# Copying the turned maxima between the two exponentials of a unit instead of ahead of both

## The chip, the cores and the metric

The kernel runs on one core of a Trainium2 chip. The metric is the device time of one execution, in microseconds (us). The profile is that of one execution. Its engines are called PE (TensorE; PEld is its loading of weights), ACT (ScalarE), DVE (VectorE), POOL (GpSimd) and SP (the DMA queue's issuer).

## The reference

A block of attention and a block of experts, each with a residual sum. What the change touches is the attention:

```python
Q, K, V = (content @ Wq), (content @ Wk), (content @ Wv)       # 4 x 1024 x 256, in 16 heads of 16
scores = jnp.einsum('bqhd,bkhd->bhqk', Q, K) / math.sqrt(HEAD_DIM)
alpha = jax.nn.softmax(scores, axis=-1)                        # over all 1024 keys
alpha = jnp.where(causal, alpha, 0)                            # the mask comes after the softmax
Y = jnp.einsum('bhqk,bkhd->bqhd', alpha, V)
x = x + layernorm(Y)
```

After it a router picks 2 of 8 experts for each of the 4096 tokens, and each expert is a 256 to 1024 to 256 MLP with GELU.

## The kernel before

The 64 pairs of batch and head are worked off in 16 groups of 4 heads (`GH = 4`, `NGR = 16`). The program position is written `p` (one group a position) and `k` (32 units a position, `U = 32`). The work of a group is a software pipeline over three positions, and each engine has a function `body(p, u, units)` which says, unit by unit, what that engine does there. Tables such as `at_m` or `at_chunk` give the unit in which each step of a group falls, counted from the start of the group's own position; a value over 31 falls in the next position or the one after it. `due(table, k)` lists what falls in unit `k`. The engines meet by semaphores only.

In each unit, for the group of the position (the *first pass*):

- PE multiplies one block of 128 queries with all 1024 keys of a head (two matmuls, line L1266, into PSUM banks 0 to 3 in turn). It may run two units ahead of DVE (`s_max`).
- DVE reduces the 128x1024 scores to the negated maximum of each query (L1706).

After each head (every 8 units) POOL splits the 8 columns of maxima in three bf16 parts (L736 to L742, `mparts`), PE turns them (L1279, a 24x128 result in rows 96 to 119 of bank 6 or 7), **ACT copies the turned maxima to `mT`** (L910, a CAST of 24x128) and counts `s_mtc`, and POOL spreads them over 24 rows of the queries' tile (L749, counts `s_ex`). So the second pass subtracts the maximum inside the matmul. The units are `at_m = [9, 17, 25, 33]`: k = 9, 17, 25 of the group's own position and k = 1 of the next one. ACT waits for `s_mtp` (PE's turning) and `s_ex` (POOL's spreading of the head before) there.

For the group before (the *second pass*), 64 chunks of 128x512, two in each unit from k = 9 on (`at_chunk = [U + LAG_B + U * c // NCH ...]`, `LAG_B = 9`):

- PE makes chunk c in bank 4 or 5 (`ebank = 4 + c % 2`, L1079; every fourth, a *corner*, L1072). It waits until exponential c - 2 is done (`s_expB`), because the two share a bank.
- ACT takes the exponential of chunk c (L926, to `et_sb`; of a corner L921, in place, with its sum in an accumulator that is read out behind it). It waits for `s_ST` (the chunk) and `s_pv` (the buffer is free).
- Each three or so units there is a *burst* on PE (L1109): the exponentials of 4 heads times the values. Bursts stand at k = 13, 16, 18, 21, 24, 26, 29 and at k = 0, 2, 5, 8, 10 of the position after. POOL multiplies the blocks on the diagonal with the mask (L770) ahead of them.

PE's own order in a unit is: turning back of results, burst, first chunk, two matmuls of the first pass, turning of the maxima (L1279), second chunk:

```python
pieces(p, u, k)
todo = due(at_chunk, k)
chunk(p, u, *todo[0])
...                       # first pass, two matmuls
...                       # turning of the maxima
for c, back in todo[1:]:
    chunk(p, u, c, back)
```

The burst of k = 2 starts a new accumulation in the bank in which the turned maxima of k = 1 lie, and waits for `s_mtc` therefore:

```python
if i == 0 and piece == 0:
    ...
    pe.wait_ge(s_mtc, min(GH * g + M_BEFORE_PV[j], NH) if isinstance(g, int) else
               GH * g + M_BEFORE_PV[j])
```

The first chunks (8 of position 1 on) begin after the projections; positions 6 to 14 are a loop of three positions run three times, and behind position 17 come the experts, whose matmuls are L1211 and L1225. The first three copies of `mT` and that of k = 1 in position 1 stand where no chunks are due yet; the other 60 have two exponentials in their unit.

Of the kernel before, what the change touches and what calls it, by code (L numbers as in the profile page):

```python
# [5 lines left out]
def sandwich(nc, x_d, wq_d, wk_d, wv_d, router_d, wfc_d, wproj_d, out_d):  # L6

    F32, BF16, I32, U32 = mybir.dt.float32, mybir.dt.bfloat16, mybir.dt.int32, mybir.dt.uint32
    ACT = mybir.ActivationFunctionType
# [38 lines left out]
    with ctx:  # L48
        def sb(name, shape, dt=F32):
            return ctx.enter_context(nc.sbuf_tensor(name, shape, dt))  # L50

        def sem(name):
            return ctx.enter_context(nc.semaphore(name))
# [10 lines left out]
        GH = 4  # L64
        NSL = 3
# [19 lines left out]
               for s in range(HSL)]  # L85
# [5 lines left out]
        NET = 3  # L91
        w0 = 0
        et_sb = [wfc[:, w0 + s * GH * 512:w0 + (s + 1) * GH * 512].rearrange("p (h q) -> p h q", h=GH)
                 for s in range(NET)]
# [34 lines left out]
        den_u = sb("den_u", [P, NSL, GH, QT // 2])  # L129
# [87 lines left out]
        def bk(i):  # L217
            return ps[:, i, :]
# [25 lines left out]
        s_dt = sem("s_dt")  # L244
# [5 lines left out]
        s_ST = sem("s_ST")  # L250
        s_expB = sem("s_expB")
        s_mask = sem("s_mask")
        s_pv = sem("s_pv")
# [91 lines left out]
        HQ = QT // 2  # L345
        HALVES = (1, 0)
        BURSTS = tuple((i, 1) for i in range(QT)) + tuple((i, 0) for i in range(HQ))
        NBU = len(BURSTS)
        NCH = (NBU + HQ) * GH
# [15 lines left out]
        at_chunk = [U + LAG_B + U * c // NCH for c in range(NCH)]  # L365
# [6 lines left out]
        def is_corner(c):  # L372

            return c % 4 == 3
# [24 lines left out]
        def due(at, k):  # L399

            return [(n, x // U) for n, x in enumerate(at) if x % U == k]
# [5 lines left out]
        def ebank(c, g):  # L407

            if isinstance(g, int) and g == NGR - 1:
                return LAST_RING[c % 4]  # L410
            return 4 + c % 2

        def live(p, back):

            return not isinstance(p, int) or 0 <= p - back < NGR
# [43 lines left out]
        def tail(at, p, k):  # L459

            if not isinstance(p, int) or p < NGR:
                return []
            return [n for n, x in enumerate(at) if x == U * (p - NGR) + k]
# [21 lines left out]
        def wait_pos(eng, s, v):  # L485

            if isinstance(v, int) and v <= 0:
                return
            eng.wait_ge(s, v)
# [32 lines left out]
        def turn_bank(hl, g):  # L522

            return 7 if isinstance(g, int) and g == 0 else 6 + HALVES[M_HALF[hl]]
# [317 lines left out]
        def _(act):  # L842
# [37 lines left out]
            def exp_gate(i):  # L880
                g = ORDER[i]
                act.wait_ge(s_d2, i + 1)
                nc.scalar.activation(gtmp[:, g * TPC:(g + 1) * TPC], gtmp[:, g * TPC:(g + 1) * TPC],
                                     ACT.Exp).then_inc(s_ex2, 1)

            def copy_x2(i, kc):
                act.wait_ge(s_x2t, KC * i + kc + 1)
                nc.scalar.copy(x2T[:, kc, :], bk(x_bank(i, kc))).then_inc(s_x2e, 1)

            def copy_l(i):  # L890
                if i == 0:
                    act.wait_ge(s_ysz, 16 * 5)
                act.wait_ge(s_lt, i + 1)
                nc.scalar.copy(lgT[:, :], bk(0)[:, 0:P]).then_inc(s_lc, 1)

            def body(p, u, units=range(U)):
                for k in units:
                    for i in tail(at_copy_l, p, k):
                        copy_l(i)
                    for n in tail(at_copy_x, p, k):  # L900
                        copy_x2(*divmod(n, KC))
                    for i in tail(at_gate, p, k):
                        exp_gate(i)
                    for hl, back in due(at_m, k):
                        if not live(p, back):
                            continue
                        h = GH * (p - back) + hl
                        act.wait_ge(s_mtp, h + 1)
                        wait_pos(act, s_ex, h)
                        nc.scalar.copy(mT[MROW:MROW + MR, :],  # L910
                                       bk(turn_bank(hl, p - back))[MROW:MROW + MR, 0:P]).then_inc(s_mtc, 1)
                    for c, back in due(at_chunk, k):
                        if not live(p, back):
                            continue
                        g = p - back
                        act.wait_ge(s_ST, NCH * g + c + 1)
                        if is_corner(c):
                            hl, i = divmod(c // 4, HQ)
                            if c < 4:
                                wait_pos(act, s_dt, g - 2)  # L920
                            nc.scalar.activation(bk(ebank(c, g)), bk(ebank(c, g)), ACT.Exp,  # L921
                                                 accum_out=den_u[:, (u - back) % NSL, hl, i:i + 1]).then_inc(s_expB, 1)
                            continue
                        b, hl = divmod(3 * (c // 4) + c % 4, GH)
                        wait_pos(act, s_pv, NBU * g + b - NET + 1)
                        nc.scalar.activation(et_sb[b % NET][:, hl, :], bk(ebank(c, g)), ACT.Exp).then_inc(s_expB, 1)  # L926

            root_c(0, 0)
            apply_c(0, 0)
# [3 lines left out]
            for c in range(NC):  # L933
                for pos in range(PER):
# [31 lines left out]
                    for p, k in early(c, pos):  # L966
                        body(p, p % NSL, (k,))
            part1(4 * NC - 1)
            act.wait_ge(s_warm, 1)
            nc.scalar.activation(warm[:, 1:2], cst0[:, 0:1], ACT.Exp).then_inc(s_warm, 1)  # L970
            groups(act, body)


# [944 lines left out]
```

## Time and profile before

| | |
|---|---|
| time, median of 3 executions | 1563.65 us (1562.59 to 1565.73) |
| time of the profiled execution | 1563.69 us |
| its span, first to last instruction | 1561.8 us |
| PE, DVE, ACT, POOL busy | 1423.3, 923.9, 805.1, 610.7 us |
| copies to `mT` (L910) | 64, of 0.258 us |
| exponentials (L926, L921) | 768 of 0.597 us and 256 of 0.584 us |
| stretch of the 60 copies that have exponentials beside them | 155 to 919 us |

A timeline row reads: start, how long, engine, line, operation, what it writes and reads, how many instructions are merged in it, and in brackets for how long the engine sat idle ahead of it and what ended that. A row of merged instructions (x2) gives the time from the first one's start to the last one's end.

### The profile page before, as it was taken

How to read it: one execution, taken by the hardware profiler on the slowest of the kernel's cores; microseconds unless marked ns; L12 is line 12 of the kernel's file. 1: busy time of each engine (PE TensorE's matmuls, PEld its weight loads, DVE VectorE, ACT ScalarE, POOL GpSimd, SP SyncE). 2: the span in 40 equal slices, each digit the busy share in tenths (PEclk: the TensorE clock that was granted, in tenths of full speed). 3: DMA queues.
4: the chain of work that ended last, by engine and by line, in shares of the span. 5: the costliest groups of instructions: out<-in, count | busy, mean ns of one | idle time of the engine just before them, and what ended most of it. 6: DMA issues, size and time to landing. Idle time of an engine off the chain costs nothing.

```text
span 1561.8 us, 31019 instructions
## 1 busy us (share of the span) xinstructions
PE 1423.3 (91%) x9774; PEld 829.3 (53%) x9775; DVE 923.9 (59%) x1740; ACT 805.1 (52%) x1717; POOL 610.7 (39%) x729
## 2 busy tenths in 40 slices
PE   6788999999999889998999998889999999999990
PEld 3444333333333223332333333689999999999990
DVE  4587788778888878887888887861111111111115
ACT  5454777777777767776777787311111111111114
POOL 2234434444444435443544441423333333333335
PEclk9999999999999999999999999999999999999995
DMA  3666622102320221132025141556666666666646
GB/s 124 153 154 142 223 41 42 30 13 41 42 40 3 42 42 27 16 42 43 16 27 96 55 136 56 158 137 193 172 183 183 176 191 173 179 188 175 187 119 219
DMA packets 100425, 167.07 MB, mean 107 GB/s; under 512 B 12400, under 2 KB 67568, under 8 KB 100304
## 3 DMA queue, kind: packets, MB, share of 16 engines
q1 hardware_dynamic: 86192, 146.08, 35.2%
q0 software_dynamic: 13632, 18.69, 7.5%
q8 instruction: 63, 1.03, 0.3%
q10 hardware_dynamic: 480, 0.79, 0.3%
q14 instruction: 58, 0.48, 0.1%
HBM read 130.76 MB, written 34.77 MB: 106 GB/s over the span
## 4 chain that ended last, share of the span: by engine, by line
PE 66%; DVE 15%; issue 9%; ACT 4%; POOL 2%; DMA 2%; DVEq 1%; ACTq 0%; POOLq 0%
PE ps L1211 16%; PE ps L1225 15%; PE ps L1109 10%; DVE negmax L1706 9%; PE ps L1079 8%; PE ps L1266 8%; ACT wfc L926 2%; PE ps L1048 2%; PE ps L1072 2%; POOL wfc L838 1%; PE ps L1253 1%; DVE x L1524 1%; PE ps L1198 1%; ACT yx L853 1%; PE ps L1057 1%
## 5 line engine op out<-in xcount | busy, mean ns | idle before, releaser
L1706 DVE TENSOR_REDUCE negmax<-ps 128x1 f32<-128x1024 f32 x512 | 607.0, 1217 | 146.3 <-PE ps L1266 143.8
L926 ACT ACTIVATE wfc<-ps 128x512 f32<-128x512 f32 x768 | 436.6, 595 | 178.0 <-PE ps L1079 169.6
L981 ACT ACTIVATE wfc<-ps 128x512 f32<-128x512 f32 x142 | 84.8, 597 | 426.8 <-PE ps L1211 426.8
L1211 PE MATMUL ps<-yx,wfc 128*128 128x128 f32 x2272 | 267.6, 276 | 5.3 <-issue 5.3
L1211 PEld LDWEIGHTS ps<-yx,wfc 128*128 128x128 f32 x2272 | 265.8, 193 | 9.5 <-issue 6.3
L770 POOL TENSOR_TENSOR wfc<-wfc,causal 128x512 f32<-128x512 f32 x128 | 162.4, 1269 | 253.6 <-ACT wfc L926 183.8
L1225 PE MATMUL ps<-arena,wfc 128*128 x1136 | 257.2, 379 | 0.8 <-issue 0.8
L826 POOL DMA_INDIRECT expert_out<-wfc,rt x71 | 112.7, 1587 | 296.9 <-DVE wfc L1670 289.2
L1225 PEld LDWEIGHTS ps<-arena,wfc 128*128 128x128 f32 x1136 | 210.3, 190 | 26.9 <-issue 1.3
L1266 PE MATMUL ps<-arena 96*128 96x512 bf16 x704 | 212.8, 384 | 9.2 <-DMA arena<-qk_parts 5.6
L1079 PE MATMUL ps<-arena 120*128 120x512 bf16 x528 | 203.4, 393 | 12.7 <-ACT wfc L926 0.4
L1109 PE MATMUL ps<-wfc 128*16 128x128 f32 (+4 forms) x2304 | 161.6, 383 | 0.5 <-POOL wfc L770 0.5
L921 ACT ACTIVATE ps<-ps 128x512 f32<-128x512 f32 x256 | 149.6, 584 | 10.9 <-PE ps L1072 2.9
L1670 DVE TENSOR_SCALAR wfc<-ps,rt 128x256 f32<-128x256 f32 x71 | 34.3, 483 | 204.1 <-PE ps L1225 204.1
L1079 PEld LDWEIGHTS ps<-arena 120*128 120x128 bf16 x528 | 50.2, 97 | 184.0 <-ACT wfc L926 114.1
L1658 DVE SCALAR_TENSOR_TENSOR rt<-yx,rt 128x1 f32 (+1 forms) x71 | 15.5, 219 | 200.7 <-PE ps L1198 200.7
L1109 PE MATMUL ps<-wfc,vone 128*17 128x128 f32 (+3 forms) x1024 | 95.4, 445 | 8.2 <-issue 7.4
L1109 PEld LDWEIGHTS ps<-wfc 128*17 128x17 f32 (+1 forms) x2304 | 60.7, 97 | 75.7 <-issue 50.2
L1079 PE MATMUL ps<-wfc 120*128 120x512 bf16 x240 | 93.0, 388 | 7.1 <-ACT wfc L926 0.8
L1266 PEld LDWEIGHTS ps<-arena 96*128 96x128 bf16 x704 | 67.7, 99 | 59.1 <-issue 13.0
L1266 PE MATMUL ps<-wfc 96*128 96x512 bf16 x320 | 95.6, 379 | 0.4
L749 POOL TENSOR_TENSOR arena<-mT,dmask 24x1024 bf16<-24x1024 bf16 x44 | 83.3, 1894 | 16.2 <-ACT mT L910 12.2
(208 smaller groups left out, 1257.4 us busy)
## 6 DMA issues: line engine op xcount, KB each, us to landing
wfc<-in_L_ffn_w_fc SPq DMA_DIRECT2D x71, 1024.0 KB, 5.3
arena<-qk_parts SPq DMA_DIRECT2D x126, 128.0 KB, 5.5
qk_parts<-x SPq DMA_DIRECT2D x32, 384.0 KB, 2.8
arena<-in_L_ffn_w_proj SPq DMA_DIRECT2D x8, 1024.0 KB, 8.0
wfc<-qk_parts SPq DMA_DIRECT2D x60, 128.0 KB, 5.6
expert_out<-rt SPq DMA_DIRECT2D x3, 1408.0 KB, 11.9
yx<-in_L_attn_content SPq DMA_DIRECT2D x8, 512.0 KB, 4.3
x<-in_L_attn_content SPq DMA_DIRECT2D x1, 4096.0 KB, 14.4
```

What stands on the lines that cost most here:

```text
L749: pool.tensor_tensor(qs[(u - back) % NSL][MROW:MROW + MR, hl, :] .rearrange("p (i q) -> p i q", i=QT), mT[MROW:MROW + MR, :].unsqueeze(1). ...
L770: pool.tensor_tensor(md_sb[b % NET], et_sb[b % NET][:, :, q:q + P], causal[:, :].unsqueeze(1).to_broadcast([P, GH, P]), ALU.mult).then_inc ...
L826: pool.indirect_dma_start(out=ys_d, in_=yslot[t % 2], in_offset=None, out_offset=bass.IndirectOffsetOnAxis(ap=tok[:, t:t + 1], axis=0), co ...
L921: nc.scalar.activation(bk(ebank(c, g)), bk(ebank(c, g)), ACT.Exp, accum_out=den_u[:, (u - back) % NSL, hl, i:i + 1]).then_inc(s_expB, 1)
L926: nc.scalar.activation(et_sb[b % NET][:, hl, :], bk(ebank(c, g)), ACT.Exp).then_inc(s_expB, 1)
L981: nc.scalar.activation(hidT[s][:, 4 * hf:4 * hf + 4, :], bk(1 + hf).rearrange("p (c t) -> p c t", c=4), ACT.Gelu).then_inc(s_ge, 1)
L1079: nc.tensor.matmul(bk(ebank(c, g)), ks[v][0:MROW + MR, hl, i * P:(i + 1) * P], qs[v][0:MROW + MR, hl, hf * 512:(hf + 1) * 512], start=True ...
L1109: ins = nc.tensor.matmul(out[32 * hl:32 * hl + rows, q0:q1], lhs, rhs, start=(i == 0 and piece == 0 and n == 0), stop=False, skip_group_ch ...
L1211: ins = nc.tensor.matmul(bk(1 + hf)[:, c * P:(c + 1) * P], w1[s][:, kc * FF + (4 * hf + c) * P:kc * FF + (4 * hf + c + 1) * P], xsT[:, kc, :],
L1225: ins = nc.tensor.matmul(bk(5 + s)[:, 0:D], hidT[s][:, c, :], arena[:, ds(off + c * D, D)], start=(c == 0), stop=(c == FC - 1))
L1266: ins = nc.tensor.matmul(bk(2 * (k % 2) + hf), qs[u][0:SROWS, hl, i * P:(i + 1) * P], ks[u][0:SROWS, hl, hf * 512:(hf + 1) * 512], start=T ...
L1706: nc.vector.tensor_reduce(negmax[:, hl % 2, i:i + 1], ps[:, 2 * (k % 2):2 * (k % 2) + 2, :], AX.XY, ALU.max, negate=True).then_inc(s_max, 1)
```

## The change

ACT's part of a unit had the copies to `mT` first and then its two exponentials. Now it has the first exponential, the copies, and the second exponential. The body of the loop over the chunks becomes a function, `exp_chunk`, which does the same as before. No instruction is added or taken away on any engine, the waits are the same, and the order of PE, DVE, POOL and SP is the same.

```diff
+                    todo = due(at_chunk, k)
+                    exp_chunk(p, u, *todo[0])
                     for hl, back in due(at_m, k):
                         if not live(p, back):
                             continue
...
                         wait_pos(act, s_ex, h)
                         nc.scalar.copy(mT[MROW:MROW + MR, :],
                                        bk(turn_bank(hl, p - back))[MROW:MROW + MR, 0:P]).then_inc(s_mtc, 1)
-                    for c, back in due(at_chunk, k):
-                        if not live(p, back):
-                            continue
-                        g = p - back
-                        act.wait_ge(s_ST, NCH * g + c + 1)
...
+                    for c, back in todo[1:]:
+                        exp_chunk(p, u, c, back)
+
+            def exp_chunk(p, u, c, back):
+                if not live(p, back):
+                    return
+                g = p - back
+                act.wait_ge(s_ST, NCH * g + c + 1)
...
```

On ACT, in position 3 from k = 0 on, these rows stood before (the CAST belongs to k = 1; `wfc` is the memory of `et_sb`, `ps` is PSUM, and the row of x3 behind the CAST is both exponentials of k = 1 and the first of k = 2):

```order
L926 ACTIVATE wfc<-ps 128x512 [waits s_pv,s_ST] x3
L921 ACTIVATE ps,den_u<-ps 128x512 [waits s_ST]
L910 CAST mT<-ps 24x128 [waits s_ex,s_mtp]
L926 ACTIVATE wfc<-ps 128x512 [waits s_pv,s_ST] x3
L921 ACTIVATE ps,den_u<-ps 128x512 [waits s_ST]
```

And in the changed kernel the same place reads (its line numbers are higher by 2 and by 5):

```order
L926 ACTIVATE ps,den_u<-ps 128x512 [waits s_ST]
L931 ACTIVATE wfc<-ps 128x512 [waits s_pv,s_ST]
L912 CAST mT<-ps 24x128 [waits s_ex,s_mtp]
L931 ACTIVATE wfc<-ps 128x512 [waits s_pv,s_ST] x2
L926 ACTIVATE ps,den_u<-ps 128x512 [waits s_ST]
```

The copy has moved behind one exponential of 128x512, and nothing else has. In each of the 60 places the instruction ahead of the copy was a corner (L921), and the next corner is two units on.

On PE, in position 3 at k = 1 and k = 2, the order is this one before and after (`vone` and `wfc` of L1109 are the stationary operands of the burst; L1079 in the first row is the first chunk of k = 1, the one behind L1279 its second, the last one the first chunk of k = 2):

```order
L1079 MATMUL ps<-arena 128x512 [waits s_expB]
L1266 MATMUL ps<-arena 128x512 [waits s_max]
L1266 MATMUL ps<-arena 128x512
L1279 MATMUL ps<-identb,mparts 24x128 [waits s_norm,s_sp]
L1079 MATMUL ps<-arena 128x512 [waits s_expB]
L1109 MATMUL ps<-wfc,vone 17x128 [waits s_expB,s_mtc,s_norm]
L1109 MATMUL ps<-wfc,vone 17x128 x3
L1109 MATMUL ps<-wfc 17x384 x4
L1109 MATMUL ps<-wfc 16x128 [waits s_mask]
L1109 MATMUL ps<-wfc 16x128 x3
L1079 MATMUL ps<-arena 128x512 [waits s_expB]
```

Nothing moved there; the row with `s_mtc` is the one that waits for the moved copy.

## Rows read from the trace of the kernel before

**Rows 1.** Page, busy time of the engines, and PE in 40 slices.
```profile
PE 1423.3 (91%) x9774; PEld 829.3 (53%) x9775; DVE 923.9 (59%) x1740; ACT 805.1 (52%) x1717; POOL 610.7 (39%) x729
PE   6788999999999889998999998889999999999990
```

**Rows 2.** Chain that ended last: whole span by engine, 190 to 915 us by line.
```profile
PE 66%; DVE 15%; issue 9%; ACT 4%; POOL 2%; DMA 2%; DVEq 1%; ACTq 0%; POOLq 0%
...
by line: PE ps L1109 19.3%; DVE negmax L1706 16.7%; issue 16.0%; PE ps L1079 15.1%; PE ps L1266 14.6%; ACT wfc L926 3.8%; PE ps L1072 3.2%; PE ps L1253 2.1%; DVE x L1524 1.8%; DVE wfc L1717 1.3%; PE ps L1279 0.8%; DVE rden L1730 0.7%; DVE s
```

**Rows 3.** Timeline of ACT, position 8, k = 1 and the start of k = 2.
```profile
495.60 0.58 ACT L921 ACTIVATE ps<-ps 128x512 f32<-128x512 f32 x1
496.09 0.19 ACT L921 ACTIVATION_READ_ACCUMULATOR ps<-ps 128x1 f32 x1
496.61 0.26 ACT L910 CAST mT<-ps 24x128 bf16<-24x128 f32 x1 [0.33 <-PE ps L1279]
496.90 1.08 ACT L926 ACTIVATE wfc<-ps 128x512 f32<-128x512 f32 x2
498.56 0.60 ACT L926 ACTIVATE wfc<-ps 128x512 f32<-128x512 f32 x1 [0.58 <-PE ps L1079]
```

**Rows 4.** Timeline of PE, the same stretch.
```profile
495.60 0.39 PE L1079 MATMUL ps<-arena 120*128 120x512 bf16 x1
...
496.35 0.23 PE L1279 MATMUL ps<-identb,mparts 128*24 128x128 bf16 x1
496.51 0.39 PE L1079 MATMUL ps<-arena 120*128 120x512 bf16 x1
496.93 0.41 PE L1109 MATMUL ps<-wfc,vone 128*17 128x128 f32 x8
...
498.13 0.39 PE L1079 MATMUL ps<-arena 120*128 120x512 bf16 x1
```

**Rows 5.** Timeline of PEld: first weight load of two bursts, k = 26 of position 7 and k = 2 of 8.
```profile
484.38 0.13 PEld L1109 LDWEIGHTS ps<-wfc,vone 128*17 128x17 f32 x8 [0.23 <-issue]
...
496.92 0.13 PEld L1109 LDWEIGHTS ps<-wfc,vone 128*17 128x17 f32 x8 [0.32 <-ACT mT L910]
```

**Rows 6.** The 64 copies (L910): who waited for them (us, times).
```profile
  POOL arena L749: 12.2, 15
...
  PEld ps L1109: 3.4, 10
```

**Rows 7.** Timeline of ACT: accumulator read then exponential; two exponentials then a copy.
```profile
480.05 0.20 ACT L921 ACTIVATION_READ_ACCUMULATOR ps<-ps 128x1 f32 x1
480.14 0.59 ACT L926 ACTIVATE wfc<-ps 128x512 f32<-128x512 f32 x1
...
944.24 1.08 ACT L926 ACTIVATE wfc<-ps 128x512 f32<-128x512 f32 x2 [0.21 <-PE ps L1079]
945.21 0.27 ACT L894 COPY rt<-ps 128x128 f32<-128x128 f32 x1
```

**Rows 8.** Timeline of ACT: the other four copies of k = 1.
```profile
393.47 0.26 ACT L910 CAST mT<-ps 24x128 bf16<-24x128 f32 x1 [0.49 <-PE ps L1279]
...
553.63 0.26 ACT L910 CAST mT<-ps 24x128 bf16<-24x128 f32 x1 [0.19 <-PE ps L1279]
...
713.30 0.26 ACT L910 CAST mT<-ps 24x128 bf16<-24x128 f32 x1 [0.70 <-PE ps L1279]
...
918.27 0.19 ACT L921 ACTIVATION_READ_ACCUMULATOR ps<-ps 128x1 f32 x1
...
918.50 0.26 ACT L910 CAST mT<-ps 24x128 bf16<-24x128 f32 x1
```

**Rows 9.** Timeline of ACT: first exponential of k = 18, position 8.
```profile
525.02 0.60 ACT L926 ACTIVATE wfc<-ps 128x512 f32<-128x512 f32 x1 [0.26 <-PE ps L1079]
```

**Rows 10.** Timeline of PE: chunk 2 of the first group (k = 10, position 1).
```profile
156.08 0.61 PE L1079 MATMUL ps<-arena 120*128 120x512 bf16 x1 [0.43 <-ACT wfc L926]
```

**Rows 11.** Timeline of POOL: first mask behind the spreading of k = 2, position 8.
```profile
500.62 1.27 POOL L770 TENSOR_TENSOR wfc<-wfc,causal 128x512 f32<-128x512 f32 x1 [1.61 <-ACT wfc L926]
```

More of the change, by code:

```diff
@@ L911, in body @@
                                        bk(turn_bank(hl, p - back))[MROW:MROW + MR, 0:P]).then_inc(s_mtc, 1)
-                    for c, back in due(at_chunk, k):
-                        if not live(p, back):
-                            continue
-                        g = p - back
-                        act.wait_ge(s_ST, NCH * g + c + 1)
[L917 to L926, printed above, removed]
+                    for c, back in todo[1:]:
[5 more added lines that the diff above has]
+                act.wait_ge(s_ST, NCH * g + c + 1)
+                if is_corner(c):
+                    hl, i = divmod(c // 4, HQ)
+                    if c < 4:
+                        wait_pos(act, s_dt, g - 2)
+                    nc.scalar.activation(bk(ebank(c, g)), bk(ebank(c, g)), ACT.Exp,
+                                         accum_out=den_u[:, (u - back) % NSL, hl, i:i + 1]).then_inc(s_expB, 1)
+                    return
+                b, hl = divmod(3 * (c // 4) + c % 4, GH)
+                wait_pos(act, s_pv, NBU * g + b - NET + 1)
+                nc.scalar.activation(et_sb[b % NET][:, hl, :], bk(ebank(c, g)), ACT.Exp).then_inc(s_expB, 1)
             root_c(0, 0)
```

## The prediction

> **What bounds the kernel now.** I read the page's busy shares first, then the chain that ended last, then the timeline around one copy. The shares say that PE is busy 91% of the span and ACT 52% [rows 1]. The chain says the same from the other side: over the span 66% of it is PE, 15% DVE and 4% ACT. In the stretch of the two passes (190 to 915 us) its parts are PE's lines, DVE's maxima with 16.7%, and ACT's exponentials with 3.8% [rows 2]. So ACT's time is worth something only where PE or DVE wait for ACT, and the change moves instructions on ACT alone. The question is who waits for what is moved.
>
> In k = 1 of position 8 the timeline shows ACT finishing the corner at 496.28 (the accumulator read, 496.09 + 0.19), then idle for 0.33 us, then copying at 496.61, the moment PE's turning ends (496.35 + 0.23 = 496.58), and only then taking the two exponentials, from 496.90 [rows 3, 4]. The chunk of the first of them was finished on PE at 495.60 + 0.39 = 495.99 [rows 4]. So ACT idles with an exponential ready, and the change puts it into that gap. All 60 copies that have exponentials beside them show such a picture: the idle time is 0.33 us in most, and the exceptions among those of k = 1 are in [rows 8].
>
> **What waits for the exponentials: nothing that would start earlier.** Chunk c + 2 needs exponential c. The first exponential of k = 1 ends now at about 497.50 (496.90 + 0.60), and PE wants to make the next chunk in its bank at 498.13, after the burst [rows 3, 4]. It is 0.63 us early already. All four copying units (k = 9, 17, 25, 1) have a burst on PE in the unit behind them (k = 10, 18, 26, 2), so this is so in all of them. On ACT itself the lead is lost at once: the next exponential (498.56) waits 0.58 us for PE's chunk as it is [rows 3]. In the other 58 units behind a copy with exponentials in both it waits for PE too, at k = 18 the least, 0.26 us [rows 9]. ACT would finish the pair earlier (the second would start at 496.95 or so instead of 497.40) and wait longer. Gain: 0. The cover is PE's burst; without it a lead of up to 0.45 us a unit would count.
>
> One place is different. At the very start (k = 9 of position 1) PE idles 0.43 us at 156.08 for the first exponential, which stands behind the copy on ACT, and the chain goes through it [rows 10]. There the exponential can run long before the turning. Gain: 0.43 us, once.
>
> **What waits for the copy.** The copy now stands behind one exponential. Where would it start? The gap of a read and an exponential behind it is 0.09 us (480.05 to 480.14). The gap of an exponential and a copy behind it is 945.21 less the start of the second of two exponentials, 944.24 + 1.08 - 0.60 = 944.72, so 0.49 us [rows 7]. That copy is of another shape (128x128), but its gap is made by the exponential ahead of it. So the copy can start 0.09 + 0.49 = 0.58 us after the start of the accumulator read, or when the turning is done, whichever is later. In position 8 that is 496.67 instead of 496.61: 0.06 us late. In general it is 0.39 us less the idle time that stands ahead of the copy now.
>
> The Trainium skill (ScalarE: Activation LUTs, What ACT_TABLE_LOAD costs) says that back-to-back ACTIVATEs overlap by about 93 ns. By that the gap would be 0.60 - 0.093 = 0.51 us and the copy 0.08 us late; with it in all the places below the sum would be about 0.3 us higher. The trace's own 0.49 is used.
>
> Who feels 0.06 us? After the copies of k = 9, 17 and 25 only POOL's spreading waits (12.2 us in 15 cases and less in the others) [rows 6]. PE needs its result with the next group's first chunks, units later, and POOL idles 1.61 us before its next mask [rows 11]. Cost: 0.
>
> After the copy of k = 1 the burst of k = 2 waits on PE, with all of PE's queue behind it: the next chunk, the first pass's matmuls and so DVE's maxima. It is tight today. The weight load of the burst starts 0.31 us after the copy's start (496.61 to 496.92), and sat 0.32 us idle with the copy as its releaser, where a burst without this wait sat idle for 0.23 [rows 3, 5]. So the wait already costs 0.09 us, and each further delay of the copy goes to PE one for one. The chain runs over PE there, so it goes to the end. There are 15 such places (positions 2 to 16):
>
> - 11 show the 0.33 us of idle time of [rows 3]: 11 x 0.06 = 0.66 us.
> - 393.47 and 713.30, with 0.49 and 0.70 us of idle time: the exponential fits, 0 [rows 8].
> - 553.63, with 0.19: 0.39 - 0.19 = 0.20 us [rows 8].
> - 918.50, where the copy follows the read at once: 918.27 + 0.58 = 918.85, so 0.35 us [rows 8]. PE has little else to do there, and I let it count in full.
>
> Sum: 0.66 + 0.20 + 0.35 - 0.43 = +0.78 us. Made against the profiled execution's own time of 1563.69 us (its span of 1561.8 and 1.9 around it; 0.04 over the median of 1563.65) this is 1564.5 us, 0.05% more. About 0.2% (3.1 us) is what a measurement of this kernel can tell from no change, so the forecast is: no difference.
>
> **Bounds of the unknown cost.** The start of an exponential behind a corner's read with a copy behind it is not in the trace in this order. From below: the copy is not late at all in the 15 places, -0.43 us, 1563.3 us. From above: the exponential starts only when the read has ended (0.19 + 0.04), and the copy only when the exponential has ended (0.60 + 0.04), 0.87 us after the read's start instead of 0.58. Then it is late by 0.68 less the idle time: 11 x 0.35, 0.19 and 0.49 for 393.47 and 553.63, 0 for 713.30, 0.64 for 918.50, together 5.2 us, 1568.9 us without the gain at the start. I take the value of [rows 7] because exponentials are seen to overlap in that way in every unit.
>
> **The rivals.**
>
> *The copy becomes a wait that counts (slower).* The mechanism is the one above: the burst of k = 2 waits for `s_mtc` behind a whole exponential. It decides from the point where the copy starts 0.24 us late instead of 0.06 in the 11 places, and by the same 0.18 more in the other four: 11 x 0.24 + 0.38 + 0.08 + 0.53 - 0.43 is 3.2 us. Its end is the upper bound, 1568.9 us, and its middle 1567.9. For it: PE's wait is tight in all 15 places [rows 3, 5], and ACT does its work in order. Against it: exponentials follow each other, and a copy an exponential, at 0.49 us with 0.60 of duration [rows 3, 7]. Chance 0.09.
>
> *The lead of ACT is worth something (faster).* ACT's exponentials hold 3.8% of the chain in 725 us, 27.5 us [rows 2]. If in 59 units the lead of 0.45 us shortened the pieces behind them by 0.08 each, this would be 4.7 us, less 0.8: 1559.8 us. It decides from 0.07 a unit. Against it: ACT waits for PE at least 0.26 us in the unit behind each of the 59 [rows 3, 9], so nothing of the lead is left where the pieces of ACT in the chain begin. Chance 0.05.
>
> *The delay is absorbed or small (no change in either way).* PE's loss may be taken back where DVE holds the chain (16.7% of it [rows 2]), and the end is then 1563.3 to 1564.5. This is within the forecast and its range.
>
> **How the numbers follow.** The forecast and what lies within 0.2% of before has 0.86, the slower rival 0.09, the faster one 0.05. The likeliest is 1564.5 us. The range of 8 in 10 takes the lower bound of the cost and the spread of single executions (before: 1562.6 to 1565.7) below it, and a good half of the way to the upper bound above it: 1562.4 to 1567.0.
>
> **What the profile after would show.** In k = 1: a single L931 directly behind the accumulator read (0.09 us after its start), the copy 0.58 us after the read's start and no idle time ahead of it, then one exponential that waits for the second chunk if at all. The idle time of ACT ahead of the copies, 0.33 us in most, goes to near nothing, and ACT's waits for PE's chunks in the unit behind grow by more than as much. PEld's wait for the copy should be about 0.38 us in the 11 places and 0.6 at the end. The distance from one copy of k = 1 to the next should grow by 0.06 us. The chain's shares should stay. It would be wrong if the copy started much more than 0.6 us behind the read, if POOL's masks came later than the bursts that need them, or if PE's burst at k = 2 waited for something else that moved.

## The result, and the profile after

The changed kernel took 1568.53 us (median of 22 executions, 1565.32 to 1570.56). The kernel before, run beside it on the same chip, took 1564.18 us (22 executions, 1562.16 to 1568.15). The medians differ by 4.35 us, and the ratio is 1.0025 with a 95% interval of 1.0018 to 1.0031, which is 2.8 to 4.8 us: slower, by more than the 0.2% below which the forecast spoke of no difference. The forecast was 0.8 us, 1564.5 us, with a range up to 1567.0.

The page of the changed kernel answers to [rows 1]. First the busy times, then the chain of its whole span.

```profile
PE 1424.3 (91%) x9774; PEld 828.8 (53%) x9775; DVE 925.4 (59%) x1740; ACT 804.9 (51%) x1717; POOL 610.6 (39%) x729
...
PE 65%; DVE 15%; issue 10%; ACT 5%; POOL 2%; DMA 2%; DVEq 1%; ACTq 0%; POOLq 0%
```

DVE is busy for 1.5 us longer than in [rows 1], though the change touched nothing on DVE. That is the first sign of a cost that the prediction did not have. The chain from 190 to 917 us, by line, answers to [rows 2]:

```profile
by line: PE ps L1114 19.2%; issue 16.7%; DVE negmax L1711 16.6%; PE ps L1084 14.7%; PE ps L1271 13.8%; ACT wfc L931 4.0%; PE ps L1077 3.1%; PE ps L1258 2.1%; DVE x L1529 2.0%; DVE wfc L1722 1.3%; DVE rden L1735 0.7%; ACT ps L926 0.7%; DVE s
```

DVE's residual sum (L1524 before, L1529 now) has gone from 1.8% to 2.0% of 725 us, some 1.5 us.

The timeline of ACT at position 8, k = 1 and the start of k = 2, answers to [rows 3]:

```profile
494.60 0.58 ACT L926 ACTIVATE ps<-ps 128x512 f32<-128x512 f32 x1
495.09 0.19 ACT L926 ACTIVATION_READ_ACCUMULATOR ps<-ps 128x1 f32 x1
495.19 0.59 ACT L931 ACTIVATE wfc<-ps 128x512 f32<-128x512 f32 x1
495.80 0.26 ACT L912 CAST mT<-ps 24x128 bf16<-24x128 f32 x1
496.08 0.60 ACT L931 ACTIVATE wfc<-ps 128x512 f32<-128x512 f32 x1
497.75 0.60 ACT L931 ACTIVATE wfc<-ps 128x512 f32<-128x512 f32 x1 [1.07 <-PE ps L1084]
```

The first exponential starts 0.10 us after the read's start, as predicted. But the copy starts 0.61 us after the exponential (495.80 less 495.19), 0.02 after its end, and not the 0.49 of [rows 7]. It stands 0.71 us behind the read instead of 0.52 (496.61 less 496.09 in [rows 3]), so it is 0.19 us late and not 0.06 (the steps below have 0.18). PEld's first weight load of the burst of k = 2 shows what that makes of the 0.32 us in [rows 5]:

```profile
496.11 0.13 PEld L1114 LDWEIGHTS ps<-wfc,vone 128*17 128x17 f32 x8 [0.50 <-ACT mT L912]
```

**Where the time is.** I took the start of each of DVE's 512 maxima in both profiles and subtracted. The difference stays flat for whole positions and moves in steps. The first row here is what the shift was before the first moved copy acts (the start of the kernel varies from one execution to the next); the steps follow.

```
place                                          steps          sum us
shift at k = 9 of position 1                                   -2.34
k = 10 to 13 of position 1                     -0.62 +0.49 +0.19  +0.06
k = 2 of positions 2-5, 7, 8, 10, 11, 13-15    11 x +0.18      +1.98
k = 18 of positions 6 to 15                    10 x +0.18      +1.83
loop edges (k = 0 to 2) of position 9          -0.34 +0.32     -0.02
  and of position 12                           +0.36 -0.38     -0.02
last maximum to the last chunk                 +0.43           +0.43
shift at the last chunk                                        +1.88
```

The rows between the two shifts add up to 4.26, and +1.88 less -2.34 is 4.22; the rest is steps of under 0.05 us and rounding. In the part of the experts another 0.24 us comes to it, and the profiled span is 1563.9 us, 2.1 over that of before. Among the profiles of this study that part differed by up to 1.9 us between kernels whose experts are the same. The 4.22 us of the attention part are close to the 4.35 us by which the medians differ. The two profiled executions differ less, because the one of the changed kernel reached k = 9 of position 1 2.34 us earlier, in a part that the change leaves alone. Neither of the two large rows was sized right: the first was forecast at 0.66 us, the second at nothing.

**The second row of steps.** POOL's spreading of the maxima (L749) and DVE's sum in k = 17 of position 8, before:

```profile
523.73 1.89 POOL L749 TENSOR_TENSOR wfc<-mT,dmask 24x1024 bf16<-24x1024 bf16 x1 [0.78 <-ACT mT L910]
...
525.03 0.87 DVE L1524 SCALAR_TENSOR_TENSOR x<-yx,rstd,x  x1
525.90 1.21 DVE L1706 TENSOR_REDUCE negmax<-ps 128x1 f32<-128x1024 f32 x1
```

and in the changed kernel:

```profile
523.10 1.89 POOL L749 TENSOR_TENSOR wfc<-mT,dmask 24x1024 bf16<-24x1024 bf16 x1 [0.96 <-ACT mT L912]
...
524.22 1.05 DVE L1529 SCALAR_TENSOR_TENSOR x<-yx,rstd,x  x1
525.27 1.21 DVE L1711 TENSOR_REDUCE negmax<-ps 128x1 f32<-128x1024 f32 x1
```

POOL waits 0.18 us longer for the copy. The sum waits on no semaphore for L749, and yet ends 0.28 us behind it both times (525.90 against 523.73 + 1.89 = 525.62; 525.27 against 523.10 + 1.89 = 524.99). It does so in all ten positions of both profiles. Its duration grows from 0.87 to 1.05 us, and the next maxima start at its end. The chain of the changed kernel runs through it (start, length, what):

```profile
523.09 1.22 DVE negmax L1711
524.31 0.97 DVE x L1529
...
525.35 0.02 DVE negmax L1711
```

Why k = 17 alone? In positions 6 to 14 POOL starts L749 0.08 us behind the copy of k = 17. At k = 9 it starts 0.82 us behind it, because POOL is busy with its mask (L770), so a copy that is late by 0.18 us would change nothing; the copy of k = 9 had 0.64 to 0.71 us of idle time ahead of it there besides. At k = 25 POOL waits for its mask too (0.39 us behind the copy). Before, at k = 9 of position 8:

```profile
510.70 1.89 POOL L749 TENSOR_TENSOR wfc<-mT,dmask 24x1024 bf16<-24x1024 bf16 x1 [0.16 <-POOL wfc L770]
```

So two theories were to be tested: the copy is held behind the exponential's end, and this goes by two paths, PE's burst at k = 2 and DVE's sum at k = 17. The rivals were that the steps come from something else in the new order, and that the copy's 0.13 us (0.62 less 0.49) lie in a copy as such.

### The profile page after: what moved, and what is told of

Same layout as the page of the kernel before. It is cut to its first block, busy times and chain, and to the rows that moved or that the text cites. A ratio compares the mean times of both kernels' runs of the same rounds, so it can differ in the third digit from the quotient of the medians.

```text
span 1563.9 us, 31019 instructions
## 1 busy us (share of the span) xinstructions
PE 1424.3 (91%) x9774; PEld 828.8 (53%) x9775; DVE 925.4 (59%) x1740; ACT 804.9 (51%) x1717; POOL 610.6 (39%) x729
## 4 chain that ended last, share of the span: by engine, by line
PE 65%; DVE 15%; issue 10%; ACT 5%; POOL 2%; DMA 2%; DVEq 1%; ACTq 0%; POOLq 0%
PE ps L1216 16%; PE ps L1230 15%; PE ps L1114 10%; DVE negmax L1711 8%; PE ps L1084 8%; PE ps L1271 7%; ACT wfc L931 2%; PE ps L1053 2%; PE ps L1077 2%; POOL wfc L838 1%; DVE x L1529 1%; PE ps L1258 1%; PE ps L1203 1%; ACT yx L853 1%; DVE wfc L1722 1%
## 5 line engine op out<-in xcount | busy, mean ns | idle before, releaser
L931 ACT ACTIVATE wfc<-ps 128x512 f32<-128x512 f32 x768 | 442.5, 595 | 201.3 <-PE ps L1084 192.7
L986 ACT ACTIVATE wfc<-ps 128x512 f32<-128x512 f32 x142 | 84.8, 597 | 426.8 <-PE ps L1216 400.1
L770 POOL TENSOR_TENSOR wfc<-wfc,causal 128x512 f32<-128x512 f32 x128 | 162.3, 1268 | 254.0 <-ACT wfc L931 185.3
L749 POOL TENSOR_TENSOR arena<-mT,dmask 24x1024 bf16<-24x1024 bf16 x44 | 83.3, 1893 | 19.1 <-ACT mT L912 16.8
```

Source lines behind the costliest of these rows:

```text
L749: pool.tensor_tensor(qs[(u - back) % NSL][MROW:MROW + MR, hl, :] .rearrange("p (i q) -> p i q", i=QT), mT[MROW:MROW + MR, :].unsqueeze(1). ...
L770: pool.tensor_tensor(md_sb[b % NET], et_sb[b % NET][:, :, q:q + P], causal[:, :].unsqueeze(1).to_broadcast([P, GH, P]), ALU.mult).then_inc ...
L986: nc.scalar.activation(hidT[s][:, 4 * hf:4 * hf + 4, :], bk(1 + hf).rearrange("p (c t) -> p c t", c=4), ACT.Gelu).then_inc(s_ge, 1)
```

## The experiments

Unless a kernel before is named, each is an edit of the changed kernel. `copy_m(p, k, heads)` is the loop of the copies, for the heads named; head 3 is the copy of k = 1, heads 0, 1 and 2 those of k = 9, 17 and 25.

### One path at a time

```diff
                     todo = due(at_chunk, k)
+                    copy_m(p, k, (3,))
                     exp_chunk(p, u, *todo[0])
-                    for hl, back in due(at_m, k):
...
+                    copy_m(p, k, [hl for hl in range(GH) if hl not in (3,)])
```

**Copy of k = 1 ahead again.** 

> The copies of k = 1 are ahead of both exponentials again; those of k = 9, 17 and 25 stay between. Theory A (two losses: the burst of k = 2 on PE waits 0.18 us longer in 11 positions and in the tail, and DVE's sum of k = 17 is held 0.18 us longer by POOL's spreading in 10 positions): the steps of the shift at k = 2 are gone, those of k = 18 stay, so about +1.9 us over before, ratio 1.0012. Rival B (the burst of k = 2 is the whole loss and the steps at k = 18 follow from it): as before, +0.1 us, 1.0000. Rival C (the loss comes from the order on ACT as such, in all four places alike): three quarters of it, +3.3 us, 1.0021.

**Copies of k = 1 and 17 ahead again** (`(1, 3)` for `(3,)`). 

> The copies of k = 1 and k = 17 are ahead of both exponentials, those of k = 9 and k = 25 stay between. Theory A: nothing is left of the loss, +0.1 us, ratio 1.0000 (0.9993 to 1.0007), and no step of over 0.05 us in the shift of DVE's maxima but at the loop's edges. Rival C (all four places alike): half of it, +2.2 us, 1.0014.

**Only that of k = 1 between** (`(0, 1, 2)`). 

> Only the copy of k = 1 is between the exponentials, the other three are ahead of both. Theory A: 11 steps of 0.18 us at k = 2 and the tail's 0.4, so +2.4 us, ratio 1.0015; DVE's sum of k = 17 takes 0.87 us as before. Rival B (all of it is the burst): the full +4.3 us, 1.0028, with steps at k = 18 too.

These three and the copy of all rows (below) ran on one chip beside 35 executions of before (1564.24 us); the row of the changed kernel is the result above, with its own executions of before. From each profile I took the steps as above, against the profile of before:

```
kernel                     median us (runs)   ratio, 95%                  11 at k=2   10 at k=18
changed                    1568.53 (22)       1.0025 [1.0018, 1.0031]     +1.98       +1.83
k = 1 ahead again          1567.22 (11)       1.0011 [1.0002, 1.0020]      0.00       +1.83
k = 1 and 17 ahead again   1565.06 (11)       1.0001 [0.9992, 1.0010]     +0.02       +0.03
only k = 1 between         1567.08 (11)       1.0016 [1.0007, 1.0025]     +2.01       +0.06
copy of 128 rows           1567.09 (12)       1.0013 [1.0003, 1.0023]     +0.61       +0.58
```

The two rows of steps come and go with the two copies, each alone, and with both copies ahead the time is that of before, though the copies of k = 9 and 25 still stand between. The medians do not contradict it: 1567.22 less 1565.06 is 2.16 us for the path of k = 17, 1567.08 less 1565.06 is 2.02 for that of k = 1 (with the tail). But each ratio is known only to about 1.4 us either way, so it is the steps that carry the argument. DVE's sum in k = 17 of position 8, with k = 1 ahead, with both ahead, and with only k = 1 between:

```profile
523.97 1.05 DVE L1533 SCALAR_TENSOR_TENSOR x<-yx,rstd,x  x1
```
```profile
524.67 0.87 DVE L1533 SCALAR_TENSOR_TENSOR x<-yx,rstd,x  x1
```
```profile
525.87 0.88 DVE L1533 SCALAR_TENSOR_TENSOR x<-yx,rstd,x  x1
```

And PEld's wait at k = 2, with k = 1 ahead and with only k = 1 between:

```profile
495.86 0.13 PEld L1118 LDWEIGHTS ps<-wfc,vone 128*17 128x17 f32 x8 [0.32 <-ACT mT L918]
```
```profile
497.75 0.13 PEld L1118 LDWEIGHTS ps<-wfc,vone 128*17 128x17 f32 x8 [0.51 <-ACT mT L918]
```

### What makes the copy start late

The rival to a hold by rows is that any copy behind an exponential starts late. Four kernels change which rows of PSUM and of `mT` ACT copies; POOL reads the same 24 rows in all. The first, with its lines joined and without the `.then_inc(s_mtc, 1)` that ends both:

```diff
-    nc.scalar.copy(mT[MROW:MROW + MR, :], bk(turn_bank(hl, p - back))[MROW:MROW + MR, 0:P])
+    nc.scalar.copy(mT[0:P, :], bk(turn_bank(hl, p - back))[0:P, 0:P])
```

**128 rows from row 0.** 

> The changed kernel, but the copy takes all 128 rows of the bank instead of rows 96 to 119 (the rows above are not read by anyone). Theory D (an instruction on ACT whose partitions start elsewhere than those of the one ahead waits for its end, others start 0.1 us before it): the copy starts 0.49 us after the exponential instead of 0.62, the steps at k = 2 and k = 18 shrink from 0.18 to about 0.05, so +1.3 us over before, ratio 1.0008. Rival E (the copy waits for the exponential's end because its semaphore comes while it is queued, or for the change from Exp to a copy to bf16): the gap stays 0.62 and the time is that of the changed kernel, 1.0025 to 1.0028.

**32 rows from row 96** (`[MROW:P]`). 

> The changed kernel with the copy on rows 96 to 127 instead of 96 to 119 (the 8 rows below are not read). Theory D1 (what holds the copy is that its partitions start at 96 where those of the exponential ahead start at 0): no overlap, the copy starts 0.025 us after the exponential's end as with 24 rows. Theory D2 (what holds it is a number of partitions that is no multiple of 32): it starts 0.1 us before the end, as with 128 rows.

**64 rows from row 64** (`[64:P]`). 

> The changed kernel with the copy on rows 64 to 127. Theory D1 (the start row decides): held as with rows 96 to 127, it starts 0.025 us after the exponential's end. Rival (only a start at 96, or a copy of one quarter of the rows, is held): 0.1 us before it.

**An extra copy of rows 0 to 23 ahead of the one of rows 96 to 119.** 

> The changed kernel with one more copy ahead of each of the 64: rows 0 to 23 of the same bank into rows 0 to 23 of mT, which nobody reads. Theory D1 (the start row holds): the extra copy starts 0.1 us before the end of the exponential ahead of it, and the copy of rows 96 to 119 behind it starts 0.025 us after the extra copy's end. Theory D3 (fewer than 128 rows hold): the extra copy too starts 0.025 us after the exponential's end. The time is not compared; the extra copy puts each copy later by about 0.26 us less the overlap, some 0.14 us by D1.

The last three have one execution each, so only the gaps and steps in their profiles are read, not their times (1568.52, 1566.74 and 1573.93 us). Timeline of ACT with the copy of 128 rows:

```profile
496.24 0.59 ACT L935 ACTIVATE wfc<-ps 128x512 f32<-128x512 f32 x1
496.72 0.27 ACT L918 CAST mT<-ps 128x128 bf16<-128x128 f32 x1
```

with 32 rows from row 96, with 64 rows from row 64:

```profile
304.13 0.59 ACT L935 ACTIVATE wfc<-ps 128x512 f32<-128x512 f32 x1
304.74 0.26 ACT L918 CAST mT<-ps 32x128 bf16<-32x128 f32 x1
```
```profile
305.44 0.59 ACT L935 ACTIVATE wfc<-ps 128x512 f32<-128x512 f32 x1
306.05 0.26 ACT L918 CAST mT<-ps 64x128 bf16<-64x128 f32 x1
```

and with the extra copy:

```profile
306.51 0.19 ACT L931 ACTIVATION_READ_ACCUMULATOR ps<-ps 128x1 f32 x1
306.60 0.59 ACT L936 ACTIVATE wfc<-ps 128x512 f32<-128x512 f32 x1
307.08 0.24 ACT L918 CAST mT<-ps 24x128 bf16<-24x128 f32 x1
307.33 0.26 ACT L919 CAST mT<-ps 24x128 bf16<-24x128 f32 x1
307.61 0.60 ACT L936 ACTIVATE wfc<-ps 128x512 f32<-128x512 f32 x1
```

A copy that starts at row 0, like the exponentials, starts 0.11 us ahead of the exponential's end (496.24 + 0.59 = 496.83 against 496.72), with 128 rows or with 24. One that starts at row 64 or 96 starts 0.02 behind it, with 24, 32 or 64 rows. The number of rows does not matter, the first row does. An exponential (row 0) behind a copy that starts at row 96 is not overlapped either: it starts 0.02 behind the copy's end (307.33 + 0.26 = 307.59 against 307.61). Whether the first row read in PSUM or the first row written decides was not separated, as the copies change both. Over all places the median gaps were -0.112 (49 pairs, 128 rows), +0.024 (48), +0.025 (50) and -0.111 us (52, the extra copy). The copy of 128 rows is late by the 0.06 us that the prediction had, and both rows of steps shrink to 0.06 a place (table above). With the extra copy, the copy of rows 96 to 119 stands 0.82 us behind the read (307.33 less 306.51), 0.30 late, and both rows of steps grow to 0.29 and 0.30 a place. So the steps follow the copy's lateness. The median of the copy of 128 rows, 1567.09, can't show this: 1.3 us over before were expected, 2.9 were measured, and the interval of its ratio reaches from 0.5 to 3.6.

The Trainium skill (VectorE: DVE Perf Modes, Two Vector instructions with no wait between them) says that a VectorE instruction with an operand that starts in another group of 32 partitions than the last operand read from (or written to) the same memory is held until every earlier VectorE instruction has finished. The page says it of VectorE only; these four kernels show the same picture on ScalarE, 0.13 us a time.

### DVE's sum moved away from POOL's spreading

If the sum is held by L749, moving it should take away the 1.83 us, and perhaps more than the change had cost. In the table `STEADY` the second sum stands at 17; the edit, made in the kernel before and in the changed one:

```diff
-        STEADY = {..., 13: ("add", 0), 17: ("add", 1),
+        STEADY = {..., 13: ("add", 0), 16: ("add", 1),
```

**Sum at 16, kernel before.** 

> The kernel before, with the second of DVE's two sums (x and the normalized rows, two operands in SBUF) in k = 16 instead of k = 17 in positions 6 to 15; in k = 16 POOL does no spreading. Theory F (that sum cannot run beside POOL's operation and is held until POOL's ends): it takes 0.475 us as its twin of k = 13 instead of 0.87, and as DVE is on the chain in that stretch, up to 10 x 0.4 us are won: -3 to -4 us, ratio 0.9975 to 0.9985. Rival G (it takes longer because of its place behind the maximum or its operands): it stays at 0.87 us and the time at 1.0000.

**Sum at 16, changed kernel.** 

> The changed kernel with the same sum moved to k = 16. Theories A and F: no steps at k = 18 and none of 0.87 us, so the gain of e8_sum_at_16 with the 2.4 us of the burst of k = 2 on top: -1.5 us against before, ratio 0.9990. Rival B (the steps at k = 18 do not come over that sum): they stay, +0.5 us or more over before.

These went the other way: 1578.30 us (5 executions, ratio 1.0094, 1.0081 to 1.0108) and 1582.44 us (4, 1.0123, 1.0108 to 1.0139), against 1563.38 us (9). The sum now meets L749 from its first moment; with the order before:

```profile
527.42 1.89 POOL L749 TENSOR_TENSOR wfc<-mT,dmask 24x1024 bf16<-24x1024 bf16 x1 [0.78 <-ACT mT L910]
...
527.59 2.00 DVE L1524 SCALAR_TENSOR_TENSOR x<-yx,rstd,x  x1
```

It ends at 529.59, again 0.28 us behind POOL's end (529.31), after 2.00 us. In the changed kernel L749 is later and the sum takes 2.19:

```profile
529.14 2.19 DVE L1529 SCALAR_TENSOR_TENSOR x<-yx,rstd,x  x1
```

I had taken k = 16 as free of L749 and misread where DVE is in its units by then. The expected gain failed; the hold itself is seen at a larger size, 1.1 us more a position. In the profile of the first kernel the ten positions make 11.4 us; the rest of the difference lies elsewhere (start, loop edges, experts), in parts that vary among the profiles here.

**Sum at 14, kernel before.** 

> The kernel before, with DVE's second sum in k = 14 instead of k = 17. With k = 16 it met the whole of POOL's spreading, since DVE runs one to two units behind the unit in which ACT copies; DVE's k = 14 lies ahead of it. Theory F (that sum is held until POOL's operation ends): it takes 0.475 us instead of 0.87, and as each 0.18 or 1.14 us more went to the end in full, 10 x 0.40 us come back: -4.0 us, ratio 0.9975. If PE becomes the bound in that stretch, less. Rival G (the place in the pipeline, not POOL's operation): no gain, 1.0000.

**Sum at 14, changed kernel.** 

> The changed kernel with the sum in k = 14. Theories A and F: no steps at k = 18; what is left of the change is the burst's 2.0 us and the tail's 0.4. So 2.4 us over the kernel before with the sum in k = 14, -1.6 us against before, ratio 0.9990. Rival B (the steps at k = 18 do not come over that sum): they stay, and the time is 4.3 us over that kernel, +0.3 us, 1.0002.

**Sum at 14 and the variance at 11, kernel before.** The variance (`var_y`, L1513, two columns) of k = 9 takes 1.38 us beside an L749, so it was moved too (`9: ("var_y", 0)` to `11`, and the step behind it, `ROOT_Y`, from 10 to 11). 

> The kernel before, with the sum in k = 14, and with DVE's small operation on the variances (L1513, 1.38 us in k = 9 under POOL's spreading, 0.17 us for its twin of k = 20) in k = 11, and POOL's root after it in k = 11 instead of 10. Theory F: it takes 0.17 us; up to 10 x 1.2 us more than with the sum alone. Where DVE is no longer the bound, PE takes over, so -8 to -16 us against before, ratio 0.990 to 0.995. Rival: POOL's root now comes late for the first sum of k = 13, and DVE waits there instead, so no more than -4 us, 0.9975.

On one chip, with 29 executions of before (1563.86 us) and 11, 12 and 11 of the three: 1565.12 us (1.0009, 1.0000 to 1.0018), 1567.78 us (1.0021, 1.0011 to 1.0030) and 1563.01 us (0.9993, 0.9983 to 1.0003). Free of L749 the sum takes 0.48 us, and DVE then waits for PE, which it did not before:

```profile
520.09 0.48 DVE L1524 SCALAR_TENSOR_TENSOR x<-yx,rstd,x  x1
...
525.26 1.23 DVE L1706 TENSOR_REDUCE negmax<-ps 128x1 f32<-128x1024 f32 x1 [0.21 <-PE ps L1266]
```

With the variance moved as well it takes 0.17 us, and the maxima wait 150.7 us for PE, where they waited 140.2 with the sum alone moved and 143.8 in the kernel before:

```profile
515.97 0.17 DVE L1513 TENSOR_SCALAR mv<-mv 128x2 f32<-128x2 f32 x1
...
  PE ps L1266: 150.7, 161
```

So the 0.4 us that the hold costs the sum in every position of before could not be turned into time: with the sum at 14 the steps were -0.57 at k = 18, but +0.46 at k = 15 and +0.16 in all at k = 24 to 26, so nothing is left. Moving the variance gave -0.63 at k = 10 and +0.48 at k = 12. The expected gain failed in all three. What the pair shows is the change's own cost: with the sum at 14 the ten steps of k = 18 are -5.55 us in the kernel before and -5.28 in the changed one, so at most 0.27 us of the 1.83 is left, while the eleven at k = 2 stay (+2.02). The two medians differ by 2.66 us. Each is known to about 1.4 us either way, so here too the steps decide. Removing the meeting of the two instructions removes the second path.

## Why the prediction was wrong

**What held.** The exponential does start in ACT's idle time of 0.33 us. The first exponential starts 0.10 us behind the read's start, so the bound that it waits for the read did not apply. The lead of ACT is worth nothing: the wait at k = 2 grew from 0.58 to 1.07 us and PE did not move, which the faster rival needed. The burst of k = 2 is tight and takes each delay of the copy one for one, in 11 places. The copy of position 6 (393.47) cost 0.04 us, that of position 12 (713.30) nothing that can be seen. Two of the prediction's own signs came out otherwise: the copy stood 0.71 us behind the read instead of 0.58, and PEld waited 0.50 us for it instead of 0.38.

**The step that failed first: the gap of an exponential and a copy.** The prediction took 0.49 us from a copy of 128x128 [rows 7], "but its gap is made by the exponential ahead of it". It is not; it is made by the copy's first row. The copy starts 0.62 us behind the exponential and is 0.18 us late, not 0.06: 11 places at 1.98 us instead of 0.66. The sign of this stood in the rows already. In [rows 3] the exponential behind the copy starts at 496.90, and the copy ends at 496.61 + 0.26 = 496.87: no overlap, where two exponentials overlap by 0.1 us (two take 1.08). All 60 exponentials behind such a copy showed it. A pair in one order tells of the pair in the other.

**The step that failed second: "only POOL's spreading waits ... Cost: 0".** The spreading is not tight for PE, and it was followed by semaphores to its own readers. But DVE's sum in k = 17 runs beside it and cannot finish before it; it stood in the profile as 0.87 us for an operation that takes 0.48 elsewhere (L1524: shortest 0.472). It cost 0.18 us in ten positions, 1.83 us, where the prediction had 0, and was in none of the rivals. The Trainium skill (SBUF — State Buffer, SBUF: two separate sides) says that GpSimd and a VectorE instruction with two SBUF inputs share a pair of ports that one holds for its whole instruction, the other being blocked. The traces agree: the sum ends 0.28 us behind L749 whether it takes 0.87, 1.05 or 2.00 us. That the ports are what it waits for is the page's account; the runs show that it waits for L749's end, and that it takes 0.48 us away from it.

**The slower rival** had the right mechanism for the first path, priced at 0.24 us a place; at 0.18 it gives 2.0 us, and with the tail 2.4, which alone would have been within 0.2%. Only both paths together pass it. That the measured 1568.53 lies between its 1566.9 and 1568.9 is luck, as nearly half of it came over DVE. Its chance of 0.09 was low for a mechanism whose one unknown, the gap, was read from an instruction of another shape.

**The tail** was 0.43 us (forecast 0.35): the copy of 918.50 [rows 8] starts 0.70 us behind the read, so 0.47 late. PE's first chunk behind that burst comes 0.47 or 0.48 us later in every profile with this copy of 24, 32 or 64 rows between the exponentials, 0.35 later with 128 rows (the forecast's size) and 0.59 with the extra copy. **Position 9** (553.63), forecast at 0.20, lies at a loop edge, where the sum of the two edges varied from -0.8 to +1.8 us among the kernels here; nothing can be read there.

**The start** (0.43 us forecast as a gain) went as predicted and was lost again in this profile. PE's idle time ahead of chunk 2 [rows 10] is gone, and the maxima of k = 10 come 3.03 us behind those of k = 9 instead of 3.65. But PE was at the lower granted clock there. The stretches of 1 us around k = 12 (engine times, then the granted clock, third number from the end of a row), before:

```profile
158.00:159.00 1.00, 1.00 (x3) 0.26 (x2) 0.80 (x1) 1.00 (x3) 0.00 (x0) 0.50 1.04 354
159.00:160.00 1.00, 1.00 (x4) 0.35 (x3) 0.72 (x1) 0.47 (x2) 0.00 (x0) 0.59 1.03 350
```

and in the changed kernel, where the same matmuls start 2.9 us earlier:

```profile
157.00:158.00 1.00, 1.00 (x4) 0.20 (x2) 0.55 (x1) 0.83 (x2) 0.00 (x0) 0.50 0.99 345
158.00:159.00 1.00, 1.00 (x9) 0.15 (x8) 0.97 (x1) 0.55 (x2) 0.00 (x0) 0.74 1.00 351
```

The clock (0.50 is 1.2 GHz) came up 5.9 us behind the maxima of k = 9 in the profile of before, and some 7 in that of after, so the pair of matmuls of k = 12 ran at the lower one:

```profile
156.93 1.06 PE L1271 MATMUL ps<-arena 96*128 96x512 bf16 x2
```

Before, the same pair ran at the higher one:

```profile
159.86 0.60 PE L1266 MATMUL ps<-arena 96*128 96x512 bf16 x2
```

The difference of 0.46 us is the step of +0.49. This is luck of the execution: the clock came up 5.8 to 6.9 us behind the maxima of k = 9 in the nine profiles where the first exponential is ahead of the copy, and 5.9 to 7.1 in the five where it is not, so its moment does not follow the order. Over all 14 profiles k = 14 came 9.32 to 9.81 us behind k = 9 in the nine (mean 9.56) and 9.74 to 10.23 in the five (mean 9.93). So the gain is some 0.37 us in the mean, close to the forecast, and absent in the pair of profiles shown.

**The sum.** From the forecast's 0.78: +1.32 (first path), +1.83 (second), +0.08 (tail), -0.20 (position 9) is 3.8 us; with the start's gain missing, as in these two profiles, 4.3. The ratio's interval is 2.8 to 4.8 us.

## What to carry to other kernels

A moved instruction's delay goes to everyone who shares something with what it releases, not only to those who wait on a semaphore: look for an operation on another engine that takes longer beside the released one than elsewhere, and ask when it will end now. And a gap between two instructions is a property of both; take it from a pair with the same first rows, if need be in the other order. A delay too small to show in one place counts when it comes 21 times on the chain.

## What the hardware showed that was not expected

- On ScalarE a copy behind an exponential overlaps it by 0.11 us when both start at row 0, and not at all (+0.02 us) when the copy starts at row 64 or 96, with 24 to 128 rows.
- VectorE's sum of 128x256 with two SBUF inputs takes 0.48 us alone and up to 2.2 us beside a POOL operation of 1.89, ending 0.28 us behind it. Its start in the profile lies ahead of the time in which it is held, so the wait is seen as duration and in no list of waits. A TENSOR_SCALAR of two columns takes 1.38 us there and 0.17 elsewhere.
- In the 14 profiles the granted clock came up from 0.50 to 1.00 between 5.8 and 7.1 us behind the maxima of k = 9 of position 1, whatever the order on ScalarE. Of the 0.61 us by which the maxima of k = 10 came earlier, 0.37 were left in the mean at k = 14.
